# Theta and phi of an attention pair written in place by GpSimd and VectorE, with one copy a half, and a third part of the stage

## The chip, the cores and the metric

The kernel runs on one core of a Trainium2 chip. The metric is the time of one execution on the device in microseconds. The kernel before took 1916.14 us, the median of three runs.

## What is computed

32 images of 128 channels by 1024 pixels go through two attention layers, each 1024 queries by 1024 keys over the pixels of one image. The first layer, the one that the change touches, is:

```python
theta = _conv1x1(x, W_theta, b_theta)      # 64 channels of 128
phi   = _conv1x1(x, W_phi, b_phi)          # 64 channels of 128
f = jnp.einsum('ndq,ndk->nqk', t, p) * scale
f = jax.nn.softmax(f, axis=-1)
attn = jnp.einsum('nqk,nck->ncq', f, g).reshape(n, c, h, w)   # g is x
return x + _conv1x1(attn, W_fuse, b_fuse)
```

The second layer is a group norm over its input, then attention with q, k and v of 128 channels, a projection and the residual. Everything is wanted in float32 accuracy, so each operand of a product is split in a high part and a remainder, and a product is two or three matmuls.

## The kernel before, in words

**Slots.** One pass of the loop has 16 slots. In slots 0 to 7 the scores of the eight row tiles (128 queries by 1024 keys) of layer 0 of one image are made, in slots 8 to 15 those of layer 1 of the image before. Each of the five engines runs through the same slots in a `body` of its own and works on a tile some slots later than TensorE: VectorE's row maxima (`maxima`, L745) and ScalarE's exponentials (`exponentials`, L631) one slot after the scores. The order of work on an engine is that of the calls in its `body`; across engines there are only semaphores. The `body` functions stand at L430 (the DMA queue of SyncE, SP), L562 (TensorE, PE), L677 (ScalarE, ACT), L840 (VectorE, DVE) and L1012 (GpSimd, POOL).

**Tiles.** Scores lie in one of three parts of PSUM (`s_ps`, order in `PART`, L37). Four tiles are a group. Tiles 1 and 2 of a group go from ACT (`pair_hi`, L663) over DVE (`take_lo`, L753) to a DMA transpose (`transposes`, L353, and `move`, L359, on SP); tile 0 goes over POOL (`copied_lo`, L973) to the same; tile 3 is transposed by TensorE itself (`transposes`, L481) once its exponential is there, in the slot after its scores. The product with the values (`values`, L490) comes six slots after the first tile of the group, a quarter a slot, so the values of the tiles 12 to 15 begin in slot 2 of the next pass and those of the tiles 0 to 3 in slot 6.

**Units.** Between the scores TensorE makes one small product a slot, by the table `UNITS` (L54): for the image after, `tp0` in slot 10 and `tp1` in slot 12 are theta (rows 0 to 63) and phi (rows 64 to 127) of pixels 0 to 511 and 512 to 1023. ACT takes a unit from PSUM to one of the two parts of `stage` (`take_unit`, L597), and waits before that until the unit that had this part before is split (`until_stage_before`, L170). `tp0` and `tp1` both have part 0, `w0` (slot 7) before them and `v1` (slot 2 of the next pass) after them too. POOL splits the unit one slot later (`split_units`, L894): high part with `scaled` (L889), remainder with `rest` (L892).

**Theta and phi.** The scores of layer 0 are two matmuls a half, with both parts of theta stacked over the partitions against phi in both halves of the partitions:

```python
mm = product(out, [(theta2[:, qs], phi2[:, 0, ks]), (theta2[:, qs], phi2[:, 1, ks])])
```

So theta's high part stands in `theta2[0:64]` and its remainder in `theta2[64:128]`, while phi's high part and remainder stand in `phi2` twice, once in each 64 partitions. POOL writes all to a buffer `tp_hl` in their own partitions, and in slot 13 SP issues four DMAs (`tp_copies`, L416, the issues at L425 to L428) that bring phi to both places and theta to both places, 1.5 MB as the profile counts them. They wait for both splits and for the last score tile of layer 0 that reads the old ones. Scores of slot 0 (`scores`, L452) wait for all four (`s_tp_copy`).

**Around slot 0.** In slot 0 TensorE's order is: scores of tile 0, the group norm's first product (`gn1`, which needs mean and variance, the end of DVE's `statistics`, L809, in slot 15), the transposes of tile 15, values. On SP the order from slot 12 is: transpose of tile 10; slot 13: reciprocals out (L382), the four copies; slot 14: reciprocals in (L393), transpose of tile 12; slot 15: transpose of tile 13; slot 0: transpose of tile 14.

Of the kernel before, what the change touches and what calls it, by code (L numbers as in the profile page):

```python
# [7 lines left out]
F32 = mybir.dt.float32  # L8
F32R = mybir.dt.float32r
# [5 lines left out]
C = 128  # L15
D = 64
# [38 lines left out]
         12: "tp1", 14: "v0"}  # L55
STAGE = {"v1": 0, "k0": 1, "k1": 0, "q0": 1, "w0": 0, "q1": 1, "tp0": 0, "w1": 1, "tp1": 0, "v0": 1}

SPLIT_LAG = {"v1": 2, "k0": 1, "k1": 1, "q0": 1, "w0": 1, "q1": 1, "tp0": 1, "w1": 1, "tp1": 1, "v0": 1}
STAGES = 2
XR_SLOT = 0  # L60
XS_SLOT = 1
X_MAX_SLOT = 7
MX_SLOT = 9
X_SLOT = 8
# [3 lines left out]
RES_SLOTS = (5, 12)  # L68
TP_COPY_SLOT = 13
TP_COPIES = 4  # L70

# [9 lines left out]
def attention_pair(nc: bass.Bass, x, w_theta_t, w_phi_t, w_fuse_t, q_w_t, k_w_t, p_w_t, v_w, vectors,  # L81
# [88 lines left out]
    def until_stage_before(it, s):  # L170
# [5 lines left out]
        return value(lambda i: count(staged_at, 0, last(i) + 1), it)  # L176

    def place(s):

        return PAIRS - 1 if s % GROUP == COPIED and s // GROUP % 2 else s % GROUP  # L180
# [24 lines left out]
    with ExitStack() as ctx:  # L205
        def sb(name, shape, dt=F32):
            return ctx.enter_context(nc.sbuf_tensor(name, shape, dt))
# [30 lines left out]
        phi2 = sb("phi2", [C, 2, N], F32R)  # L238

        tp_hl = sb("tp_hl", [C, 2, N], F32R)  # L240
        q_hi, q_lo = sb("q_hi", [C, N], F32R), sb("q_lo", [C, N], F32R)
# [74 lines left out]
        s_den = sem("den_scaled_ready")  # L316
        s_tp_copy = sem("theta_phi_copied")
        s_split_hi = sem("unit_split_hi")
# [24 lines left out]
        def _(sp):  # L343
# [71 lines left out]

            def tp_copies(it, s):  # L416
                if s != TP_COPY_SLOT or not here(mx_at, it, MX_SLOT):
                    return
                sp.wait_ge(s_split, before(staged_at, it, s))
                sp.sem_inc(s_carrier)  # L420

                sp.wait_ge(s_scores, before(tile_at, it, PHASE))
                sp.sem_inc(s_carrier)
                theta_hl, phi_hl = (tp_hl[rows, :, :].bitcast(F32) for rows in (slice(0, D), slice(D, C)))
                sp.dma_start(phi2[0:D, :, :].bitcast(F32), phi_hl).then_inc(s_tp_copy, 16)  # L425
                sp.dma_start(phi2[D:C, :, :].bitcast(F32), phi_hl).then_inc(s_tp_copy, 16)
                sp.dma_start(theta2[0:D, :].bitcast(F32), theta_hl[:, 0, :]).then_inc(s_tp_copy, 16)  # L427
                sp.dma_start(theta2[D:C, :].bitcast(F32), theta_hl[:, 1, :]).then_inc(s_tp_copy, 16)  # L428

            def body(it):  # L430
                for s in range(SLOTS):
                    reciprocals_in(it, s)
                    transposes(it, s)
                    reciprocals_out(it, s)
                    image_loads(it, s)
                    stores(it, s)
                    tp_copies(it, s)

# [5 lines left out]
        def _(pe):  # L444
# [7 lines left out]
            def scores(it, s, half):  # L452
                if not here(tile_at, it, s):
                    return
                if half == 0:

                    last = part_before(it.like, s)
                    if last is not None and copied_at(last):
                        pe.wait_ge(s_exp, until_part_before(tile_at, it, s))
                    if last is not None and crossed_at(last):  # L460
                        pe.wait_ge(s_pair, until_part_before(crossed_at, it, s))
                    if last is not None and turned_at(last):
                        pe.wait_ge(s_tlo, until_part_before(turned_at, it, s))
                    if s == 0:
                        pe.wait_ge(s_tp_copy, 16 * TP_COPIES * before(mx_at, it, 0))
                    if s == PHASE:
                        pe.wait_ge(s_split, before(staged_at, it, 7))
                    if s == PHASE + GROUP:
                        pe.wait_ge(s_split, before(staged_at, it, 9))
# [118 lines left out]
        def _(act):  # L588
# [8 lines left out]
            def take_unit(it, s):  # L597
# [11 lines left out]

                act.wait_ge(s_split, until_stage_before(it, s))  # L610
                to = stage[:, STAGE[name], :]
                if name[0] == "v":
# [87 lines left out]
        def _(dve):  # L700
# [119 lines left out]
            def x_maxima(it, s):  # L820
                if s != X_MAX_SLOT or not here(x_at, it, X_SLOT):
# [6 lines left out]
                                        apply_absolute_value=True).then_inc(s_x_max, 1)  # L828

            def bound_to_scale(it, s):  # L830
                s = s - 1
                if here(mx_at, it, s):
                    value_scale(0, before(mx_at, it, s) + 1)
# [6 lines left out]
            def body(it):  # L840
                for s in range(SLOTS):
                    take_bounds(it, s)
                    maxima(it, s)
                    normalised(it, s)
                    take_lo(it, s)
                    reciprocals(it, s)
                    bound_to_scale(it, s)
                    x_maxima(it, s)
                    statistics(it, s - 2, 0)
                    statistics(it, s - 1, 1)  # L850
# [27 lines left out]
        def _(pool):  # L878
# [15 lines left out]
            def split_units(it, s):  # L894
# [7 lines left out]
                if name[0] == "t":  # L902

                    pool.wait_ge(s_tp_copy, 16 * TP_COPIES * or_none(before(mx_at, it, s) - 1))
                    hi, lo = (tp_hl[:, n, half * HALF:(half + 1) * HALF] for n in range(2))
                    hi_read = hi.bitcast(F32)
# [150 lines left out]
```

## Time and profile before

| | us |
|---|---|
| median of three runs | 1916.14 (1911.53 to 1922.02) |
| the profiled execution, whole | 1910.44 |
| its span, first to last instruction | 1908.6 |
| TensorE's matmuls, busy | 1738.8 |
| VectorE, ScalarE, GpSimd, busy | 1383.4, 1404.0, 1379.7 |

Of TensorE's idle time the largest piece by far is ended by the DMA that fills theta. The clock that TensorE was granted was 0.961 of full speed in the mean. A table of busy time says little here, as all engines are between 72% and 91%; what counts is the piece of a pass in which TensorE stands still, and what came last there. TensorE's `gn1` product occurs once a pass, so its start times mark the passes: those at 81.7 and 1794.3 us are 30 passes apart.

### The profile page before, as it was taken

To read this page: it belongs to the slowest core of one execution; us is meant where nothing else is said; L and a number is where in the kernel's file an instruction comes from. 1 tells how busy PE (TensorE), PEld (TensorE's weight loads), DVE (VectorE), ACT (ScalarE), POOL (GpSimd) and SP (SyncE) were. 2 spreads that over 40 slices of the span, in tenths; PEclk is the share of its full clock that TensorE was granted. 3 is DMA by queue.
4 is the path that set the end of the run, shared out by engine and by line. 5 is a ranking of instruction groups with operands and counts; after the bars stand their busy time and mean duration, and the time that the engine had idled before them with its cause. 6 is when DMAs were issued, how large, how long until landed. Compare 5 with 4: busy or idle time off the path is not lost.

```text
span 1908.6 us, 34400 instructions
## 1 busy us (share of the span) xinstructions
PE 1738.8 (91%) x8970; PEld 1141.4 (60%) x8970; DVE 1383.4 (72%) x1541; ACT 1404.0 (74%) x2088; POOL 1379.7 (72%) x1449
## 2 busy tenths in 40 slices
PE   4699999999999999999999999999999999999996
PEld 3456656666665666656666565666666666656653
DVE  4478777778777778777778777778777777777764
ACT  3378777778777778777778777778777777877764
POOL 3468766778777778776778776778776778876754
PEclk9799999999999999999999999999999999999999
DMA  4588888898988988888988898888888988888874
GB/s 91 117 161 167 173 177 173 173 176 163 179 178 172 176 174 168 179 176 173 179 173 168 178 180 172 184 173 171 173 178 176 187 169 177 168 170 175 173 140 94
DMA packets 861110, 319.89 MB, mean 168 GB/s; under 512 B 823328, under 2 KB 824224, under 8 KB 856992
## 3 DMA queue, kind: packets, MB, share of 16 engines
q1 hardware_dynamic: 861088, 319.64, 84.0%
q8 instruction: 9, 0.15, 0.0%
q14 instruction: 13, 0.11, 0.0%
HBM read 50.86 MB, written 17.04 MB: 36 GB/s over the span
## 4 chain that ended last, share of the span: by engine, by line
PE 42%; issue 14%; DMA 11%; POOL 11%; ACT 9%; SPq 6%; DVE 4%; POOLq 0%; ACTq 0%; DVEq 0%
PE o_ps L449 15%; PE s_ps L449 15%; DMA theta<-tp_hl 10%; PE m_ps L449 6%; PE s_ps L487 6%; SPq L427 3%; ACT s_ps L649 3%; POOL x_lo L892 2%; ACT et L659 2%; DVE den_scaled L779 2%; ACT h_hi L628 2%; ACT e L649 2%; DVE neg_max L750 1%; POOL tp_hl L892 1%; POOL y_sb L996 1%
## 5 line engine op out<-in xcount | busy, mean ns | idle before, releaser
L750 DVE TENSOR_REDUCE neg_max<-s_ps 128x1 f32<-128x1024 f32 x512 | 625.5, 1222 | 226.4 <-PE s_ps L449 222.6
L449 PE MATMUL o_ps<-et,v_hi 128*128 128x512 f16 x2048 | 709.9, 388 | 20.5 <-issue 10.8
L449 PE MATMUL s_ps<-phi,theta 128*128 128x512 f32 x1024 | 343.3, 460 | 108.9 <-DMA theta<-tp_hl 99.7
L449 PE MATMUL o_ps<-et,v_lo 128*128 128x512 f16 x1024 | 396.7, 387 | 0.0
L449 PEld LDWEIGHTS o_ps<-et,v_hi 128*128 128x128 f16 x2048 | 206.5, 101 | 265.7 <-issue 83.3
L767 DVE SCALAR_TENSOR_TENSOR pair<-s_ps,pair 128x1024 f16<-128x1024 f32 x256 | 312.0, 1219 | 38.5 <-ACT pair L674 37.2
L649 ACT ACTIVATE s_ps<-s_ps,neg_max 128x1024 f32<-128x1024 f32 x256 | 278.0, 1086 | 79.5 <-DVE neg_max L750 77.9
L449 PEld LDWEIGHTS s_ps<-phi,theta 128*128 128x128 f32 x1024 | 201.8, 201 | 184.1 <-DMA theta<-tp_hl 102.6
L892 POOL TENSOR_TENSOR pair<-e_copied,pair 128x1024 f16<-128x1024 f32 x128 | 274.2, 2142 | 22.2 <-ACT pair L672 22.2
L761 DVE SCALAR_TENSOR_TENSOR et<-s_ps,et 128x1024 f16<-128x1024 f32 x128 | 156.8, 1225 | 180.0 <-ACT et L659 180.0
L674 ACT ACTIVATE pair<-s_ps 128x1024 f16<-128x1024 f32 x256 | 262.2, 1024 | 17.6
L449 PE MATMUL s_ps<-k_hi,q_hi 128*128 128x512 f32 x512 | 248.6, 486 | 4.5 <-POOL q_lo L892 2.1
L449 PE MATMUL s_ps<-k_hi,q_lo 128*128 128x512 f32 x512 | 202.7, 396 | 0.0
L449 PE MATMUL s_ps<-k_lo,q_hi 128*128 128x512 f32 x512 | 200.8, 392 | 0.0
L659 ACT ACTIVATE et<-s_ps 128x1024 f16<-128x1024 f32 x128 | 131.1, 1024 | 71.8 <-PE s_ps L487 65.4
L649 ACT ACTIVATE e<-s_ps,neg_max 128x1024 f32<-128x1024 f32 x128 | 142.8, 1115 | 48.4 <-DVE neg_max L750 48.2
L487 PE MATMUL s_ps<-ident_sb,e 128*128 128x128 f32 x1024 | 155.0, 301 | 12.1 <-ACT e L649 12.1
L487 PEld LDWEIGHTS s_ps<-ident_sb,e 128*128 128x128 f32 x1024 | 135.5, 159 | 37.9 <-ACT e L649 27.0
L892 POOL TENSOR_TENSOR v_lo<-stage,v_hi 128x512 f16<-128x512 f32 x128 | 148.2, 1158 | 10.7
L649 ACT ACTIVATE e_copied<-s_ps,neg_shifted 128x1024 f32<-128x1024 f32 x128 | 143.0, 1117 | 4.1
L449 PEld LDWEIGHTS o_ps<-et,v_lo 128*128 128x128 f16 x1024 | 102.7, 100 | 71.5 <-issue 5.0
L672 ACT ACTIVATE pair<-e_copied 128x1024 f16<-128x1024 f32 x128 | 135.3, 1057 | 9.2
(130 smaller groups left out, 2849.2 us busy)
## 6 DMA issues: line engine op xcount, KB each, us to landing
phi<-tp_hl SPq DMA_DIRECT2D x64, 512.0 KB, 5.4
rden_row<-rden_dram SPq DMA_DIRECT2D x128, 256.0 KB, 4.5
xs<-in_x SPq DMA_DIRECT2D x32, 512.0 KB, 4.8
theta<-tp_hl SPq DMA_DIRECT2D x64, 256.0 KB, 7.1
out_y<-y_sb SPq DMA_DIRECT2D x64, 256.0 KB, 3.5
et<-pair SPq DMA_TRANSPOSE x384, 4.5
rden_dram<-rden SPq DMA_DIRECT2D x128, 2.0 KB, 2.0
w_f<-in_w_fuse_t SPq DMA_DIRECT2D x1, 64.0 KB, 2.4
```

The source lines that it names most:

```text
L427: sp.dma_start(theta2[0:D, :].bitcast(F32), theta_hl[:, 0, :]).then_inc(s_tp_copy, 16)
L449: mm = pe.matmul(out, lhs_t, rhs, start=start and n == 0, stop=stop and n == len(terms) - 1)
L487: mm = pe.transpose(s_ps[:, part(t), kb * P:(kb + 1) * P], e[:, kb * P:(kb + 1) * P], ident[:, :])
L628: nc.scalar.activation(h_hi[:, :], x1[:, :], ACT.Identity, scale=gn_a[:, 0:1], bias=gn_b[:, 0:1]).then_inc(s_hhi, 1)
L649: nc.scalar.activation(to[:, :], s_ps[:, r, :], ACT.Exp, bias=bias, accum_out=den[:, g, t % GROUP:t % GROUP + 1]).then_inc(s_exp, 1)
L659: nc.scalar.activation(et[:, t // GROUP % 4, TURNED, 0:KB, :], s_ps[:, part(t), :].rearrange("k (b q) -> k b q", b=KB), ACT.Copy, scale=E_ ...
L672: nc.scalar.activation(pair[:, r, 0, :], e_copied[:, :], ACT.Copy).then_inc(s_copied_hi, 1)
L674: nc.scalar.activation(pair[:, r, 0, :], s_ps[:, part(t), :], ACT.Copy, scale=E_SCALE).then_inc(s_pair_hi, 1)
L750: nc.vector.tensor_reduce(neg_max[:, t % 4:t % 4 + 1], s_ps[:, part(t), :], AX.X, ALU.max, negate=True).then_inc(s_max, 1)
L761: nc.vector.scalar_tensor_tensor(out=blocks[:, KB:2 * KB, :], in0=s_ps[:, part(t), :].rearrange("k (b q) -> k b q", b=KB), scalar=E_SCALE, ...
L767: nc.vector.scalar_tensor_tensor(out=pair[:, r, 1, :], in0=s_ps[:, part(t), :], scalar=E_SCALE, in1=pair[:, r, 0, :], op0=ALU.mult, op1=AL ...
L892: nc.gpsimd.tensor_tensor(out, in_, hi, ALU.subtract).then_inc(sem, 1)
```

## The change

Theta and phi are written to `theta2` and `phi2` themselves, and `tp_hl` is gone. For each half POOL writes theta's high part to `theta2[0:64]` with one more instruction, then splits the whole unit into `phi2` (its rows 64 to 127 are phi; rows 0 to 63 get theta's parts, which nobody reads). DVE computes theta's remainder into `theta2[64:128]`, in slots 12 (`tp0`) and 14 (`tp1`). SP copies phi's two parts from rows 64 to 127 to rows 0 to 63 with one DMA of 256 KB a half, in slots 12 (`tp0`) and 13 (`tp1`). POOL's writing waits until the last score tile of layer 0 is made. `tp0` gets a part of `stage` of its own, a third one, and ACT waits for DVE's remainders before it overwrites a part from which they are computed.

```diff
-STAGE = {... "tp0": 0, "w1": 1, "tp1": 0, "v0": 1}
+STAGE = {... "tp0": 2, "w1": 1, "tp1": 0, "v0": 1}
-STAGES = 2
+STAGES = 3
-TP_COPY_SLOT = 13
-TP_COPIES = 4
+THETA_LO_SLOTS = {12: "tp0", 14: "tp1"}
+PHI_SLOTS = {12: "tp0", 13: "tp1"}
...
-            def tp_copies(it, s):
-                if s != TP_COPY_SLOT or not here(mx_at, it, MX_SLOT):
-                    return
-                sp.wait_ge(s_split, before(staged_at, it, s))
+            def phi_copies(it, s):
+                unit = unit_slot(PHI_SLOTS.get(s))
+                if unit is None or not here(tp_at, it, unit):
+                    return
+                half = int(UNITS[unit][-1])
+                cols = slice(half * HALF, (half + 1) * HALF)
+                sp.wait_ge(s_split, before(staged_at, it, unit) + 1)
                 sp.sem_inc(s_carrier)
-
-                sp.wait_ge(s_scores, before(tile_at, it, PHASE))
-                sp.sem_inc(s_carrier)
-                theta_hl, phi_hl = (tp_hl[rows, :, :].bitcast(F32) for rows in (slice(0, D), slice(D, C)))
-                sp.dma_start(phi2[0:D, :, :].bitcast(F32), phi_hl).then_inc(s_tp_copy, 16)
-                sp.dma_start(phi2[D:C, :, :].bitcast(F32), phi_hl).then_inc(s_tp_copy, 16)
-                sp.dma_start(theta2[0:D, :].bitcast(F32), theta_hl[:, 0, :]).then_inc(s_tp_copy, 16)
-                sp.dma_start(theta2[D:C, :].bitcast(F32), theta_hl[:, 1, :]).then_inc(s_tp_copy, 16)
+                sp.dma_start(phi2[0:D, :, cols].bitcast(F32), phi2[D:C, :, cols].bitcast(F32)).then_inc(s_phi, 16)
...
                     if s == 0:
-                        pe.wait_ge(s_tp_copy, 16 * TP_COPIES * before(mx_at, it, 0))
+                        pe.wait_ge(s_phi, 16 * before(tp_at, it, 0))
+                        pe.wait_ge(s_theta_hi, before(tp_at, it, 0))
+                        pe.wait_ge(s_theta_lo, before(tp_at, it, 0))
...
                 act.wait_ge(s_split, until_stage_before(it, s))
+                if name in ("tp0", "v1"):
+
+                    act.wait_ge(s_theta_lo, before(tp_at, it, s))
...
+            def theta_lo(it, s):
+                unit = unit_slot(THETA_LO_SLOTS.get(s))
+                if unit is None or not here(tp_at, it, unit):
+                    return
+                name, n = UNITS[unit], before(tp_at, it, unit)
+                half = int(name[-1])
+                cols = slice(half * HALF, (half + 1) * HALF)
+                dve.wait_ge(s_theta_hi, n + 1)
+                nc.vector.tensor_tensor(theta2[D:C, cols], stage[0:D, STAGE[name], :], theta2[0:D, cols].bitcast(F32),
+                                        ALU.subtract).then_inc(s_theta_lo, 1)
...
                     bound_to_scale(it, s)
+                    theta_lo(it, s)
                     x_maxima(it, s)
...
-                    pool.wait_ge(s_tp_copy, 16 * TP_COPIES * or_none(before(mx_at, it, s) - 1))
-                    hi, lo = (tp_hl[:, n, half * HALF:(half + 1) * HALF] for n in range(2))
+                    pool.wait_ge(s_scores, before(tile_at, it, PHASE))
+                    cols = slice(half * HALF, (half + 1) * HALF)
+                    scaled(theta2[0:D, cols], src[0:D, :], 1.0, 1.0, ALU.mult, ALU.mult).then_inc(s_theta_hi, 1)
+
+                    hi, lo = phi2[:, 0, cols], phi2[:, 1, cols]
                     hi_read = hi.bitcast(F32)
```

`phi_copies` takes the place of `tp_copies` at the end of SP's slot.

## Rows read from the trace of the kernel before

**Rows 1.** The page: span, and TensorE's busy time, share, instructions.

```profile
span 1908.6 us, 34400 instructions
PE 1738.8 (91%) x8970; PEld 1141.4 (60%) x8970; DVE 1383.4 (72%) x1541; ACT 1404.0 (74%) x2088; POOL 1379.7 (72%) x1449
```

**Rows 2.** TensorE's waits from 81.7 to 1794.3 us: total us, times, longest.

```profile
PE s_ps L449 <- DMA theta<-tp_hl: 91.0, 30, 4.5
PE o_ps L449 <- issue: 5.8, 9, 1.0
```

**Rows 3.** Stretches: length, busy by engine (PE first), granted clock, DMA share, GB/s.

```profile
81.70:1794.30 1712.60, 1604.16 (x8357) 1059.27 (x8356) 1284.53 (x1405) 1312.13 (x1949) 1290.20 (x1348) 0.97 0.87 174
425.50:483.50 58.00, 55.15 (x282) 36.14 (x281) 42.81 (x47) 43.86 (x65) 43.15 (x45) 0.94 0.85 172
1394.80:1450.70 55.90, 51.95 (x282) 34.32 (x281) 41.95 (x47) 43.94 (x65) 43.11 (x45) 1.00 0.89 178
```

**Rows 4.** TensorE's waits in the single pass from 1394.8 to 1450.7 us.

```profile
PE s_ps L449 <- DMA theta<-tp_hl: 2.8, 1, 2.8
PE o_ps L449 <- issue: 1.1, 2, 0.7
```

**Rows 5.** Timeline around slot 0: TensorE's start, length, line, tiles, idle before.

```profile
820.58 0.38 PE L449 MATMUL o_ps<-et,v_hi 128*128 128x512 f16 x1
824.47 1.20 PE L449 MATMUL s_ps<-phi,theta 128*128 128x512 f32 x4 [3.51 <-DMA theta<-tp_hl]
825.64 1.52 PE L487 MATMUL s_ps<-ident_sb,e 128*128 128x128 f32 x8
```

**Rows 6.** Timeline of SP's queue, same pass.

```profile
814.90 0.51 SPq L425 DMA_DIRECT2D phi<-tp_hl  x1
...
818.01 2.50 SPq L428 DMA_DIRECT2D theta<-tp_hl  x1
820.77 1.08 SPq L393 DMA_DIRECT2D rden_row<-rden_dram  x1
822.10 8.64 SPq L368 DMA_TRANSPOSE et<-pair  x3
```

**Rows 7.** The first copy of phi: duration of its issue, and time to landing.

```profile
L425 SPq DMA_DIRECT2D phi<-tp_hl x32: 472/508/549, 19.4 to 1782.9; - x32
...
DMA to landing us min/median/max: 4.2/4.2/4.3
```

**Rows 8.** The page's DMA issues: KB each, median us from issue to landing.

```profile
rden_row<-rden_dram SPq DMA_DIRECT2D x128, 256.0 KB, 4.5
```

**Rows 9.** Timeline of GpSimd, slots 11 to 14 of the same pass.

```profile
807.20 0.62 POOL L889 TENSOR_SCALAR tp_hl<-stage 128x512 fp32r<-128x512 f32 x1
...
812.37 1.28 POOL L892 TENSOR_TENSOR tp_hl<-stage,tp_hl 128x512 fp32r<-128x512 f32 x1
816.17 1.27 POOL L986 TENSOR_TENSOR x<-x,xr 128x512 f32<-128x512 f32 x1 [2.53 <-DVE x L804]
817.40 2.14 POOL L892 TENSOR_TENSOR pair<-e_copied,pair 128x1024 f16<-128x1024 f32 x1
```

**Rows 10.** Timeline of VectorE, same pass.

```profile
812.54 1.13 DVE L779 SCALAR_TENSOR_TENSOR den_scaled<-den,v_scale,e_factors 128x4 f32<-128x4 f32 x1
...
815.04 1.05 DVE L804 TENSOR_TENSOR x<-o_ps,rden_row 128x512 f32<-128x512 f32 x1
816.01 1.22 DVE L750 TENSOR_REDUCE neg_max<-s_ps 128x1 f32<-128x1024 f32 x1
...
818.68 0.68 DVE L814 BATCH_NORM_STATS2 stats<-x 128x6 f32<-128x512 f32 x1
...
820.02 1.23 DVE L750 TENSOR_REDUCE neg_max<-s_ps 128x1 f32<-128x1024 f32 x1 [0.29 <-issue]
...
829.48 0.21 DVE L779 SCALAR_TENSOR_TENSOR den_scaled<-den,v_scale,e_factors 128x4 f32<-128x4 f32 x1
```

**Rows 11.** Timeline of ScalarE, same pass: the end of tile 15's exponential.

```profile
822.38 0.19 ACT L649 ACTIVATION_READ_ACCUMULATOR e<-s_ps,neg_max 128x1 f32 x1
```

More of the change, by code:

```diff
@@ L55 @@
          12: "tp1", 14: "v0"}
-STAGE = {"v1": 0, "k0": 1, "k1": 0, "q0": 1, "w0": 0, "q1": 1, "tp0": 0, "w1": 1, "tp1": 0, "v0": 1}
+STAGE = {"v1": 0, "k0": 1, "k1": 0, "q0": 1, "w0": 0, "q1": 1, "tp0": 2, "w1": 1, "tp1": 0, "v0": 1}
 SPLIT_LAG = {"v1": 2, "k0": 1, "k1": 1, "q0": 1, "w0": 1, "q1": 1, "tp0": 1, "w1": 1, "tp1": 1, "v0": 1}
-STAGES = 2
+STAGES = 3
 XR_SLOT = 0
@@ L62 @@
 X_MAX_SLOT = 7
-MX_SLOT = 9
 X_SLOT = 8
@@ L176, in until_stage_before, with unit_slot @@
         return value(lambda i: count(staged_at, 0, last(i) + 1), it)
+    def unit_slot(name):
+        return next((s for s, unit in UNITS.items() if unit == name), None)
     def place(s):
@@ L238, in attention_pair @@
         phi2 = sb("phi2", [C, 2, N], F32R)
-        tp_hl = sb("tp_hl", [C, 2, N], F32R)
         q_hi, q_lo = sb("q_hi", [C, N], F32R), sb("q_lo", [C, N], F32R)
@@ L316, in attention_pair @@
         s_den = sem("den_scaled_ready")
-        s_tp_copy = sem("theta_phi_copied")
+        s_theta_hi, s_theta_lo = sem("theta_hi_ready"), sem("theta_lo_ready")
+        s_phi = sem("phi_twice")
         s_split_hi = sem("unit_split_hi")
@@ L436, in body @@
                     stores(it, s)
-                    tp_copies(it, s)
+                    phi_copies(it, s)
             iterations(sp, body, first=-1)
```

## The prediction

> **What bounds the kernel now.** I read the page first. TensorE is busy for 91% of 1908.6 us and the three others for 72% to 74% [rows 1], so the question is what TensorE's idle time is made of. The table of its waits over the 30 steady passes (81.7 to 1794.3 us) answers: 91.0 us in 30 waits, one a pass, are ended by the DMA that fills theta; the next kind is 5.8 us in nine waits [rows 2]. So 3.03 us a pass, and all in one place. The timeline of TensorE shows the place: after the values of slot 15, issued at 820.58 and some 0.4 us long, it stands for 3.51 us before the scores of slot 0 [rows 5].
>
> The wait has a second price. The table by stretches gives the granted clock: 1.00 in some passes, 0.94 in others, 0.97 over all 30 [rows 3]. In the pass shown the transposes right after the wait take 1.52 us for eight [rows 5]; it is TensorE at 1.2 instead of 2.4 GHz, just after it stood still. A clock of 0.97 over 1712.6 us costs 51 us (43 to 60, as the figure is rounded), 1.7 us a pass.
>
> A pass now takes 1712.6 / 30 = 57.09 us. Without the theta wait and at full clock 57.09 - 3.03 - 1.7 = 52.36 us are left. A single pass says the same: the one from 1394.8 us ran at 1.00, took 55.9 us and had 2.8 us of theta wait [rows 3, 4], which leaves 53.1, of which 1.1 us are two waits at values products with no cause shown [rows 4]. So TensorE's own work in a pass is close to 52.0 us, and that is the floor.
>
> **What the change removes.** The last of the four copies is issued at 818.01, lasts 2.50 us on SP's queue, and TensorE goes on at 824.47; the first had been issued at 814.90 [rows 5, 6]. All four are serial on one queue, and phi's first, 512 KB, lands 4.2 us after its issue [rows 7]. Now only phi's copy of 256 KB a half is left. The one of `tp0` goes in slot 12, the one of `tp1` in slot 13 at the place of the four. The second needs POOL's split of `tp1`, whose remainder now ends at 812.37 + 1.28 = 813.65 [rows 9]. POOL gets one more high part before each half; 0.62 us is the row of a 128x512 one [rows 9], and two of them move that end to about 814.9. So the second copy is issued near 815.0, where the first of the four was. I take its landing at 4.2 us as phi's first, which is twice its size [rows 7], and 4.5 us as another 256 KB DMA [rows 8] for the upper end: it lands at 819.2 to 819.5. TensorE wants it at about 821.0 (820.58 and the last values). It is 1.5 us early, and the theta wait goes to nothing. Half the partitions make no difference to that: phi's first copy also runs over 64 of them. The Trainium skill (SBUF — State Buffer, on concurrent DMAs and ports) says that only a transfer over all 128 partitions reaches all ports, so that a copy from 64 to 64 partitions would be slow for its size; the row of 4.2 us is such a copy and has this in it.
>
> SP's queue gets free earlier too. Behind the four copies were the reciprocals (820.77) and the three transposes of the tiles 12 to 14, from 822.10 for 8.64 us [rows 6]. Tile 12 is ready when POOL's remainder ends, 817.40 + 2.14 = 819.5 [rows 9].
>
> **What it adds, on POOL.** Two high parts, 2 x 0.62 us a pass. POOL stood idle for 2.53 us ahead of L986 in slot 14 [rows 9], which comes right behind, so nothing on the path moves. If that cover were gone, 1.24 us would go into the mean and variance that `gn1` needs. The added wait for the scores of layer 0 is over since slot 8. Behind it on POOL stands only work of slot 11 and later. ACT's waits for theta's remainders look at work done at least four slots before (`v1` in slot 2 after slot 14), and `tp1` no longer waits for the split of `tp0`, which was not TensorE's wait in any row; I count both as nothing.
>
> **What it adds, on DVE.** Two subtractions of 64x512, both operands in SBUF. No row has this form. From below: a two-operand instruction on 128x4 takes 0.21 us [rows 10]. From above: L804 on 128x512, with an operand in PSUM and a strided one, takes 1.05 us [rows 10]. Nearest is the statistics instruction, 128x512 out of SBUF, at 0.68 us [rows 10], and I take 0.7. By the formula in the Trainium skill (VectorE: DVE Perf Modes, fp32 `tensor_tensor`) it would be 0.69 us; no run here shows it yet.
>
> The one in slot 12 lies before tile 12's maximum, whose exponential waits for ACT anyway: nothing. The one in slot 14 follows L804 directly, at 816.0, and behind it are, in order, tile 14's maximum (816.01), tile 13's remainder, the statistics (818.68), and tile 15's maximum (820.02) [rows 10]. The 0.29 us that DVE had to spare there cover part of it; tile 15's exponential, now over at 822.38 + 0.19 = 822.57 [rows 11], moves to about 823.0.
>
> **What is late next.** TensorE starts slot 0 at about 821.0. From the scores to the transposes of tile 15, with `gn1` between, it took 825.64 - 824.47 = 1.17 us [rows 5], so it stands before the transposes at 822.15. These need that exponential, over at 823.0, and some 0.1 us for the semaphore. So a wait of 0.95 us appears, now hidden under the theta wait (without the subtraction it would be 0.5). Its bounds are 0.5 and, if DVE gives way to POOL once (1.27 us, below), 2.2. `gn1` needs the statistics at about 820.3: no wait. The rest of DVE's and ACT's chain is a little closer behind TensorE for the next slots, and the transposes of the tiles 12 to 14 must have landed by slot 2. The pass from 1394.8 shows what happens where the clock does not fall: 1.1 us of waits at values products, which a slower TensorE did not have [rows 4]. They can be the landing of transposes. Over all passes the waits other than theta's that are in the 52.36 are already 0.4 us. I add 0.7 us for the passes that had none of them; the bounds are 0 and 1.5.
>
> **Sum.** 52.36 + 0.75 (the 0.95 less some 0.2 that such waits cost now) + 0.7 = 53.8 us a pass, against 57.09: 3.3 us, times 30 = 99 us. The first theta wait is longer, outside these 30 passes, with POOL's split the last before it: there the end moves from 824.47 to 819.2 as above, less 0.6 for POOL: 4.7 us. Together 104 us. The profiled execution took 1910.44 us, of which 1.8 are outside its span; 1910.4 - 104 = 1806. The median of the runs shown is 5.7 us higher. I say 1808.
>
> **The rivals.**
> *Nothing new waits.* DVE's subtraction fits in gaps, the transposes come in time, because the DMA queues carry 0.5 MB instead of 1.5 MB: 52.4 us a pass, 4.7 x 30 + 4.7 = 146 us less, 1765. For it: the DMA share was 0.87 and falls. Against it: the exponential of tile 15 is late by 0.5 us even in the rows as they stand. 0.12.
> *The clock falls all the same.* A wait and a lower clock go together [rows 5], but not strictly: the pass from 1394.8 us ran at 1.00 with a wait of 2.8 us in it [rows 3, 4], and the mean wait of a pass is no longer than 3.03 us. If about 1 us before the transposes is enough, 1.7 us a pass are kept: 55.5 us, 1910.4 - 48 - 5 = 1857. Against it: waits up to 1.0 us at values products are in passes with a clock of 1.00. 0.15.
> *DVE and POOL block one another (slower).* The 128x4 instruction that takes 0.21 us alone took 1.13 us from 812.54, and ended at 813.67, just when POOL's subtraction begun at 812.37 ended, 813.65 [rows 9, 10]. So DVE with both operands in SBUF waits for a POOL instruction in progress. If the subtraction of slot 14 lost not once but to L986 and to L892 right after it (816.17 to 819.5), it would be 3.5 us late; tile 15's exponential with it, so TensorE would wait 4.5 us in slot 0, with the low clock again: 52.36 + 4.3 + 0.7 + 1.7 = 59.1, 2.0 us a pass more, 1910 + 55 = 1965. It decides from a delay of 2.4 us on. Against it: L804 of DVE ends at 816.09 and releases L986 at 816.17, so DVE's next instruction starts first; and DVE got in when one POOL instruction had ended [rows 9, 10]. The Trainium skill (SBUF — State Buffer, on who interferes with whom) has it as an exclusive lock, held for the whole instruction by whichever starts first, for DVE with two SBUF inputs against a POOL instruction that reads SBUF; the rows of 1.13 against 0.21 us agree. 0.06.
> *It doesn't do what it says.* The second copy lands too late, and the theta wait becomes a phi wait of about the same length: it would have to take 9.5 us from its issue at 815.0, where the rows show 4.2 and 4.5. About 1905. 0.04.
>
> **How the numbers follow.** The forecast has 0.63, with the rivals 0.12, 0.15, 0.06 and 0.04. A measurement of this kernel can tell about 0.5%, 10 us, from no change. Faster by more: 0.63 + 0.12 + 0.15 = 0.90; within: 0.04; slower: 0.06. The forecast's own bounds: waits of 0.5 and 0 give 52.7 us a pass, 1775; 2.2 and 1.5 give 55.9, 1870. For 8 times in 10 I take 1770 to 1860, which holds the forecast, most of the clock rival, and leaves out most of the case with nothing new.
>
> **What would show it.** Each step: TensorE's waits no longer name a DMA of theta, and phi's copies are released well before slot 0; a wait of 0.5 to 1.5 us a pass stands before the transposes (L487 of before), ended by ACT's exponential; DVE's new instruction lasts about 0.7 us and starts within 0.1 us of the end of L804 in slot 14; POOL's idle time ahead of L986 shrinks by about 1.2 us; the granted clock is 0.99 or more; a pass takes 53.8 us. The prediction would be wrong if the clock falls with a wait of 1 us, or if values products in the slots 2 and 6 wait for transposes for more than 1.5 us a pass.

## The result, and the profile after

The changed kernel takes 1783.43 us (median, 1780.63 to 1784.94) beside 1916.43 us for the kernel before: a ratio of 0.9303, 95% interval 0.9275 to 0.9332. It is 7% faster, where 1808 us was forecast. The profiled execution took 1780.63 us against 1910.44, so it is there that 129.8 us have to be found.

The page of the changed kernel, first lines, then the DMA issues with their median time to landing:

```profile
span 1778.8 us, 34679 instructions
PE 1686.0 (95%) x8970; PEld 1112.1 (63%) x8970; DVE 1414.7 (80%) x1605; ACT 1399.3 (79%) x2088; POOL 1442.2 (81%) x1513
...
phi<-phi SPq DMA_DIRECT2D x64, 256.0 KB, 3.1
...
et<-pair SPq DMA_TRANSPOSE x384, 4.5
```

TensorE's waits over the 30 steady passes, which now run from 76.9 to 1668.9 us, and the row of that stretch (length, busy by engine, granted clock, DMA share, GB/s):

```profile
PE s_ps L487 <- ACT e L652: 16.4, 44, 1.2
PE o_ps L447 <- issue: 11.9, 23, 1.3
PE o_ps L447 <- POOL k_lo L907: 2.5, 2, 1.3
```
```profile
76.90:1668.90 1592.00, 1556.07 (x8358) 1032.09 (x8357) 1311.90 (x1465) 1307.40 (x1948) 1349.05 (x1408) 1.00 0.85 167
```

Beside [rows 2, 3]: the 91.0 us of theta waits are gone and no DMA of phi has taken their place. The transposes by TensorE now wait 16.4 us for ScalarE's exponential: 11.6 us of it in slot 0, before those of tile 15 (29 waits, 0.39 us a pass), the rest in slot 4, before those of tile 3. Values products wait 11.9 us with no cause in this view: 5.6 us in slot 2 and 6.3 us in slot 6. The clock is 1.00 instead of 0.97. A pass takes 1592.0 / 30 = 53.07 us instead of 57.09, which is 120.6 of the 129.8 us. The start of the first of these passes moved from 81.7 to 76.9 us, 4.8 us. The piece behind the last of them is 109.9 instead of 114.3 us long; the clock that fell after the last theta wait belongs to that piece, so it is the same gain once more.

Slot 0 of one pass, to be held against [rows 5, 6, 9 to 11]: first TensorE, then SP, then GpSimd, VectorE and ScalarE, each with start, length, line and tiles, and in brackets the idle time before.

```profile
819.42 1.27 PE L447 MATMUL s_ps<-phi,theta 128*128 128x512 f32 x4
820.54 0.28 PE L530 MATMUL m_ps<-mean_var,group_avg_sb 128*128 128x2 f32 x2
821.17 1.09 PE L487 MATMUL s_ps<-ident_sb,e 128*128 128x128 f32 x8 [0.35 <-ACT e L652]
...
828.06 0.39 PE L447 MATMUL o_ps<-et,v_hi 128*128 128x512 f16 x1
```
```profile
810.90 0.76 SPq L426 DMA_DIRECT2D phi<-phi  x1
...
813.59 0.60 SPq L426 DMA_DIRECT2D phi<-phi  x1
...
818.34 6.59 SPq L370 DMA_TRANSPOSE et<-pair  x3
```
```profile
812.22 1.28 POOL L907 TENSOR_TENSOR phi<-stage,phi 128x512 fp32r<-128x512 f32 x1
814.29 1.77 POOL L1004 TENSOR_TENSOR x<-x,xr 128x512 f32<-128x512 f32 x1 [0.79 <-DVE x L807]
```
```profile
811.34 0.29 DVE L782 SCALAR_TENSOR_TENSOR den_scaled<-den,v_scale,e_factors 128x4 f32<-128x4 f32 x1
...
813.14 1.07 DVE L807 TENSOR_TENSOR x<-o_ps,rden_row 128x512 f32<-128x512 f32 x1
814.24 0.69 DVE L841 TENSOR_TENSOR theta<-stage,theta 64x512 fp32r<-64x512 f32 x1
...
818.57 1.22 DVE L753 TENSOR_REDUCE neg_max<-s_ps 128x1 f32<-128x1024 f32 x1 [0.29 <-PE s_ps L447]
```
```profile
820.92 0.19 ACT L652 ACTIVATION_READ_ACCUMULATOR e<-s_ps,neg_max 128x1 f32 x1
```

TensorE goes from slot 15 to the scores of slot 0 without a gap. The second copy is issued when GpSimd's split ends (812.22 + 1.28 = 813.50, issue at 813.59) and lands 3.1 us later, at 816.7, 2.7 us early. The exponential of tile 15 ends at 821.11 and the transposes start at 821.17. The three DMA transposes behind the copies begin 2.2 us before `gn1` and take 6.59 us of SP's queue, where they took 8.64; this pass is at the low end, over the 30 passes the median is 7.2 us, against 8.5 us before.

### The profile page after: what moved, and what is told of

The parts are those of the page before. It is cut to its first block, busy times and chain, and to the rows that moved or that the text cites. A ratio compares the mean times of both kernels' runs of the same rounds, so it can differ in the third digit from the quotient of the medians.

```text
span 1778.8 us, 34679 instructions
## 1 busy us (share of the span) xinstructions
PE 1686.0 (95%) x8970; PEld 1112.1 (63%) x8970; DVE 1414.7 (80%) x1605; ACT 1399.3 (79%) x2088; POOL 1442.2 (81%) x1513
## 4 chain that ended last, share of the span: by engine, by line
PE 66%; issue 13%; DVE 8%; ACT 7%; POOL 2%; DMA 1%; ACTq 0%; SPq 0%; DVEq 0%; POOLq 0%
PE o_ps L447 26%; PE s_ps L447 22%; PE m_ps L447 11%; PE s_ps L487 7%; DVE neg_max L753 3%; DVE pair L770 2%; ACT e L652 2%; ACT s_ps L652 2%; ACT h_hi L631 1%; DVE stats L817 1%; ACT et L662 1%; DMA et<-pair 1%; DVE den_scaled L782 1%; DVE x L807 0%; DVE theta L841 0%
## 5 line engine op out<-in xcount | busy, mean ns | idle before, releaser
L447 PE MATMUL o_ps<-et,v_hi 128*128 128x512 f16 x2048 | 696.6, 382 | 28.3 <-issue 18.2
L447 PE MATMUL o_ps<-et,v_lo 128*128 128x512 f16 x1024 | 389.8, 381 | 0.0
L447 PEld LDWEIGHTS o_ps<-et,v_hi 128*128 128x128 f16 x2048 | 202.9, 99 | 269.8 <-issue 78.4
L447 PE MATMUL s_ps<-phi,theta 128*128 128x512 f32 x1024 | 332.1, 447 | 12.5 <-ACT e_copied L652 4.8
L447 PEld LDWEIGHTS s_ps<-phi,theta 128*128 128x128 f32 x1024 | 197.2, 194 | 73.5 <-ACT e_copied L652 6.2
L487 PE MATMUL s_ps<-ident_sb,e 128*128 128x128 f32 x1024 | 136.1, 276 | 23.3 <-ACT e L652 22.4
L487 PEld LDWEIGHTS s_ps<-ident_sb,e 128*128 128x128 f32 x1024 | 114.8, 140 | 51.4 <-ACT e L652 40.5
```

The costliest lines, as they stand in the source:

```text
L447: mm = pe.matmul(out, lhs_t, rhs, start=start and n == 0, stop=stop and n == len(terms) - 1)
L487: mm = pe.transpose(s_ps[:, part(t), kb * P:(kb + 1) * P], e[:, kb * P:(kb + 1) * P], ident[:, :])
```

## The experiments

**First question: was it the wait?** The theory on record books the gain as theta wait plus clock. The rival is that the copies cost something else as well: bytes in the DMA queues and time of SP's queue ahead of the transposes. Four runs on one chip, with the kernel before at 1906.08 us.

**e1, the kernel before without the wait.** Edit to the kernel before (the scores of tile 0 read constant tiles, so this part of the computation is left out):

```diff
-                    if s == 0:
+                    if s == 1:
                         pe.wait_ge(s_tp_copy, 16 * TP_COPIES * before(mx_at, it, 0))
...
+                if s == 0:
+                    mm = product(out, [(theta_f[:, qs], phi_f[:, 0, ks]), (theta_f[:, qs], phi_f[:, 1, ks])])
```

> The kernel before with its four copies as they are, but TensorE waits for them in slot 1 instead of slot 0: the scores of tile 0 of layer 0 are computed from constant tiles (theta_f, phi_f), so their content is left out of the computation. Traffic, GpSimd's and VectorE's work and SP's order stay those of before. Theory (the gain is the wait of 3.0 us a pass and the clock that it costs): the theta wait is gone or under 0.5 us, the clock is 0.99, a pass takes 53.0 to 54.0 us, the median 1785 to 1815 us. Rival (the gain comes from 1 MB a pass less in the DMA queues and from SP's queue being free 4 us earlier, so that transposes land in time): a pass stays above 55.5 us, the median above 1860, with waits at the values products of slot 2 instead.

Measured: 1913.06 us, ratio to before 1.002 (0.9992 to 1.0048). The theory missed by 100 us, and the rival's bound was kept. TensorE's waits from 73.6 to 1851.7 us, SP's queue, and TensorE in the same pass (`gn1` at 879.84):

```profile
PE o_ps L451 <- issue: 96.4, 30, 3.8
PE s_ps L491 <- ACT e L654: 9.8, 31, 1.3
```
```profile
875.38 2.53 SPq L430 DMA_DIRECT2D theta<-tp_hl  x1
878.17 1.10 SPq L395 DMA_DIRECT2D rden_row<-rden_dram  x1
879.53 8.12 SPq L370 DMA_TRANSPOSE et<-pair  x3
```
```profile
890.39 0.39 PE L451 MATMUL o_ps<-et,v_hi 128*128 128x512 f16 x1 [3.03 <-issue]
```

The theta wait is gone from the steady passes, and a wait of 3.2 us a pass stands in slot 2, before the first values product of the tiles 12 to 15. The clock is no better than before, 0.95 from 82 to 1660 us. This view names no cause ("issue"). The view of the line of the DMA transposes does: over the same stretch it lists who waited for them, and narrowed to the last of the three in this pass it gives its start, 885.9 us, and its time to landing:

```profile
  PE o_ps L451: 96.8, 31
```
```profile
L370 SPq DMA_TRANSPOSE et<-pair x1: 1765/1765/1765, 885.9 to 885.9; - x1
DMA to landing us min/median/max: 4.3/4.3/4.3
```

It lands at 890.2 us and TensorE goes on at 890.39. In each of the 27 passes of e1 between 76 and 1670 us for which all is in the trace that product starts 0.18 to 0.21 us after this landing. The same holds in all 14 kernels of this document: their traces have 306 waits at values products between 76 and 1670 us that are put down to "issue" or to a DMA transpose, and each ends 0.18 to 0.38 us after a DMA transpose lands.

**e2, half a MB of traffic added.** The changed kernel with two copies of 256 KB from a constant tile to a spare one behind phi's second copy; their own semaphore is awaited one pass later.

```diff
+                if half == 1:
+                    sp.dma_start(spare[0:D, :].bitcast(F32), spare_src[:, 0, :].bitcast(F32)).then_inc(s_spare, 16)
+                    sp.dma_start(spare[D:C, :].bitcast(F32), spare_src[:, 1, :].bitcast(F32)).then_inc(s_spare, 16)
```

> The changed kernel plus the two DMAs of 256 KB that theta had before, from a constant tile to a spare one, issued behind phi's second copy in slot 13 and awaited by nobody but themselves a pass later. Theory (the wait, not the traffic): SP's queue is blocked for some 4.4 us as before, ends at about where the transposes of slot 14 start now, and the transposes land a little later: +0 to +1 us a pass, median 1783 to 1815. Rival (the traffic and the queue were the price): back to 1860 or more.

Measured: 1784.87 us, 0.9351 (0.9313 to 0.9388), no change of time that can be told from the changed kernel. In the trace the bytes are not free: the three transposes behind them take 7.7 us of SP's queue in the median instead of 7.2, the last lands 0.4 us later against `gn1`, and the wait in slot 2 grows from 0.2 to 0.4 us a pass. The expected blocking of SP by 4.4 us did not come: the two issues took 0.49 and 0.63 us, where theta's in the kernel before took 1.88 and 2.50 behind two copies of 512 KB. So the length of an issue on SP was no property of the copy alone; it went with what had been queued in front of it.

**e3, theta in place, phi by two DMAs of 512 KB.** In slot 13, from a buffer:

```diff
-PHI_SLOTS = {12: "tp0", 13: "tp1"}
+PHI_SLOTS = {13: "tp1"}
...
-                sp.dma_start(phi2[0:D, :, cols].bitcast(F32), phi2[D:C, :, cols].bitcast(F32)).then_inc(s_phi, 16)
+                sp.dma_start(phi2[0:D, :, :].bitcast(F32), tp_hl[D:C, :, :].bitcast(F32)).then_inc(s_phi, 16)
+                sp.dma_start(phi2[D:C, :, :].bitcast(F32), tp_hl[D:C, :, :].bitcast(F32)).then_inc(s_phi, 16)
```

> Theta in place as in the changed kernel, but phi from a buffer by the two DMAs of 512 KB of the kernel before, both in slot 13. By the rows of before the second lands 7.1 us after the first is issued. The theory: first issue 5.8 us before TensorE wants slot 0, so a phi wait of about 1.4 us in slot 0, which hides the wait for tile 15's exponential (0.5 us): +0.9 us a pass, and with a clock of 0.99 the median is near 1812; if a wait of 1.4 us is enough for the clock to fall, 1.7 to 1.9 us more a pass, near 1868. Rival (only theta's copies were late): as the changed kernel, 1783.

Measured: 1834.56 us, 0.9624 (0.9579 to 0.967). TensorE's largest wait and the stretch from 82 to 1660 us:

```profile
PE s_ps L449 <- DMA theta<-tp_hl: 82.3, 27, 4.5
```
```profile
PE s_ps L451 <- DMA phi<-tp_hl: 54.2, 28, 2.3
```
```profile
82.00:1660.00 1578.00, 1507.59 (x8058) 996.66 (x8057) 1272.06 (x1411) 1263.24 (x1879) 1300.16 (x1357) 0.99 0.85 172
```

The first line is the kernel before in the same stretch, the others are e3. The phi wait is 1.9 us a pass, not 1.4, and the clock stays at 0.99; the time lies between the two that were expected. So theta in place with phi left to the DMA is worth a little over half of the gain.

**e4, phi's second copy one slot later.** `PHI_SLOTS = {12: "tp0", 14: "tp1"}`, behind the transpose of tile 12.

> The changed kernel with phi's second copy in slot 14 of SP instead of 13, so behind the transpose of tile 12, which waits for GpSimd's remainder. Theory (what matters is where the last copy stands in SP's order against slot 0): it is issued 7 us later, lands 17.7 to 19 us after the mark at which slot 0 wants it at 13.4, a phi wait of 4.3 to 5.5 us, the clock falls in most passes, a pass takes 58 to 60 us and the median is 1930 to 1990, slower than before. Rival (SP's order does not matter, the smaller copies do): within 1% of the changed kernel.

Measured: 1956.51 us, 1.0257 (1.0215 to 1.0299): slower than the kernel before, by the order on SP alone. SP and TensorE in one pass, and the stretch:

```profile
831.37 1.84 SPq L370 DMA_TRANSPOSE et<-pair  x1
833.40 1.01 SPq L426 DMA_DIRECT2D phi<-phi  x1
```
```profile
837.34 2.07 PE L447 MATMUL s_ps<-phi,theta 128*128 128x512 f32 x4 [4.54 <-DMA phi<-phi]
```
```profile
82.00:1660.00 1578.00, 1445.34 (x7496) 959.56 (x7495) 1189.12 (x1316) 1173.68 (x1745) 1211.10 (x1260) 0.96 0.76 151
```

The wait and the clock came as expected (4.5 us a pass, 0.96).

**Second question: what is the second price of the copies?** After e1 the theory was changed: behind the theta wait lies a second one of the same length, for the transposes that are queued behind the copies; both must go. e5 puts the missing 1 MB back into the changed kernel, awaited by nobody:

```diff
+                    sp.dma_start(spare[0:D, :, :].bitcast(F32), spare_src[:, :, :].bitcast(F32)).then_inc(s_spare, 16)
+                    sp.dma_start(spare[D:C, :, :].bitcast(F32), spare_src[:, :, :].bitcast(F32)).then_inc(s_spare, 16)
```

> The changed kernel plus two DMAs of 512 KB from a constant tile to a spare one, issued on SP behind phi's second copy in slot 13 and awaited by nobody until a pass later: the 1.5 MB a pass of the kernel before, with nothing waiting for the added part. The first theory (only the theta wait counted) fell with the run in which TensorE no longer waited for theta and then stood 3.2 us a pass in slot 2. New theory: behind the theta wait lay a second one of the same length, for the transposes of the tiles 12 to 14, which are queued behind the copies; 1 MB more in front of them brings it back: their issue ends 7 us or more after gn1 instead of 4.4, a wait of 2 to 3.5 us in slot 2, a pass of 55.5 to 57.5 us, median 1860 to 1915. Rival (the run with 0.5 MB more cost nothing, so traffic in front of the transposes is free, and what the wait-free variant of before lost came from elsewhere): under 1800.

Measured: 1917.15 us, 1.0062 (1.0041 to 1.0083), 2 us above the expected range; the clock is 0.95 from 82 to 1660 us. All of the gain is gone, with theta and phi in place and nobody waiting for the added bytes. SP and TensorE (`gn1` at 876.75):

```profile
871.32 0.49 SPq L433 DMA_DIRECT2D spare<-spare_src  x1
871.85 0.62 SPq L434 DMA_DIRECT2D spare<-spare_src  x1
872.73 2.15 SPq L398 DMA_DIRECT2D rden_row<-rden_dram  x1
875.13 9.49 SPq L373 DMA_TRANSPOSE et<-pair  x3
```
```profile
887.41 0.60 PE L456 MATMUL o_ps<-et,v_hi 128*128 128x512 f16 x1 [3.06 <-issue]
```

The transposes begin 1.6 us before `gn1`, where they began 2.2 us before it in the changed kernel, and last 9.49 us. Over the passes the medians are 10.0 instead of 7.2 us of SP's queue, and the last lands 10.6 instead of 7.5 us after `gn1`. So of the 3.0 us of delay 0.6 are SP getting to them later, and the rest is that they are slower with 1.5 MB in front of them. The wait in slot 2 is 3.2 us a pass and ends 0.2 us after that landing, as in e1.

**e11, the same 1 MB in slot 10.** The two issues moved from slot 13 to slot 10 of SP, ahead of the transposes of the tiles 8 to 10 (`if s != 10 or not here(mx_at, it, 9): return` in a function of their own).

> The same two added DMAs of 512 KB as in the run with full traffic, but issued on SP in slot 10, before the transposes of the tiles 8 to 10, where the trace of the changed kernel shows a DMA share of 0.6. Theory (it is the place of the bytes, in front of the transposes of the tiles 12 to 14 that layer 0's short slots give little time, and not their number): the wait in slot 2 does not come back, 0 to +1 us a pass, median 1783 to 1815. Rival (the DMA engines are near full over the whole pass, so 1 MB more costs wherever it stands): 1860 to 1915, as with the copies in slot 13.

Measured: 1836.91 us, 0.9646 (0.9608 to 0.9685). Neither expectation holds. The trace shows both at work:

```profile
824.20 0.52 SPq L436 DMA_DIRECT2D spare<-spare_src  x1
824.78 0.58 SPq L437 DMA_DIRECT2D spare<-spare_src  x1
826.81 10.76 SPq L373 DMA_TRANSPOSE et<-pair  x3
```
```profile
840.32 0.52 PE L460 MATMUL o_ps<-et,v_hi 128*128 128x512 f16 x1 [1.38 <-issue]
```

Again the transposes behind the added bytes are stretched, to 10.76 us here, and in the median to 11.2 us where the same group took 7.1 in the changed kernel; the last of them lands 3.5 us later against `gn1`. The values product of their group, now in slot 14, waits for 1.38 us here and 1.6 us a pass in the mean, so this group had almost 2 us to spare and the one of slot 2 had nothing. 1 MB cost in both places in front of a group, and the place decided how much.

**Third question: the new wait before the transposes of tile 15.** Theory: it is set by VectorE's chain from slot 13 on. e6 to e8 ran on one chip (before: 1906.82 us), e9 and e10 on a second (1909.36 us), e12 on a third with e11 (1903.02 us).

**e6, VectorE's subtraction of slot 14 twice**, the first time into a spare tile, `if half == 1:` in front of the old one.

> The changed kernel with VectorE's subtraction of slot 14 done twice, the first time into a spare tile. Theory (VectorE's chain from slot 14 to tile 15's maximum ends TensorE's wait in slot 0, 0.53 us a pass now): 0.69 us more on VectorE become 0.5 to 0.7 us more a pass, median 1799 to 1806. Rival (VectorE has slack there): 1783, within 0.3%.

Measured: 1826.85 us, 0.9587 (0.9563 to 0.9611), some 43 us more than the changed kernel where 16 to 23 were expected. VectorE and GpSimd in one pass, and TensorE's wait from 82 to 1660 us:

```profile
828.11 1.07 DVE L808 TENSOR_TENSOR x<-o_ps,rden_row 128x512 f32<-128x512 f32 x1
829.10 0.68 DVE L843 TENSOR_TENSOR spare<-stage,theta 64x512 fp32r<-64x512 f32 x1
829.79 1.67 DVE L845 TENSOR_TENSOR theta<-stage,theta 64x512 fp32r<-64x512 f32 x1
```
```profile
829.25 1.66 POOL L1008 TENSOR_TENSOR x<-x,xr 128x512 f32<-128x512 f32 x1 [0.29 <-DVE x L808]
830.87 2.59 POOL L911 TENSOR_TENSOR pair<-e_copied,pair 128x1024 f16<-128x1024 f32 x1
```
```profile
PE s_ps L488 <- ACT e L653: 68.5, 58, 2.2
```

The first subtraction, right behind L808, goes through in 0.68 us and GpSimd's L1008 is held up (1.66 us, where it took 1.27 [rows 9] and 1.77 in the changed kernel). The second is asked for with L1008 under way: it takes 1.67 us and ends at 831.46, while GpSimd's ends at 830.91, so 0.55 of its 0.69 us of work lie behind that. GpSimd's next is stretched in turn, from 2.14 to 2.59. So one more instruction of 0.69 us added 1.7 us to VectorE's chain, and the wait in slot 0 rose by 1.6 us a pass, from 0.39 to 2.0.

**e7, GpSimd's high part of theta in slot 13 twice**, the first time into a spare tile.

> The changed kernel with GpSimd's high part of theta in slot 13 done twice, the first time into a spare tile: +0.61 us. Theory (GpSimd's addition is covered by its idle time of 0.6 to 0.8 us ahead of the addition of the residual in slot 14, and phi's copy lands 1.5 us early): 1783, within 0.3%. Rival (phi's copy or the mean and variance are at the edge): +0.3 us or more a pass, median 1792 or more.

Measured: 1789.18 us, 0.9387 (0.936 to 0.9414). Against the 0.9303 and 0.9327 of the changed kernel that is slower by 0.6% to 0.9%. One of the two intervals of the changed kernel overlaps with this one, so the times alone say little, but the trace shows that the theory (within 0.3%) missed. GpSimd was still idle for 0.58 us ahead of L1007, so it was not late. VectorE and GpSimd in slot 13:

```profile
812.96 1.22 DVE L783 SCALAR_TENSOR_TENSOR den_scaled<-den,v_scale,e_factors 128x4 f32<-128x4 f32 x1
```
```profile
812.97 0.61 POOL L905 TENSOR_SCALAR theta<-stage 64x512 fp32r<-64x512 f32 x1
813.55 0.62 POOL L905 TENSOR_SCALAR spare<-stage 64x512 fp32r<-64x512 f32 x1
```

VectorE's instruction of 0.21 us on 128x4 takes 1.22 us here and ends at 814.18, with GpSimd's second instruction (814.17); in the changed kernel it took 0.29. All its operands lie in SBUF, and it stands at the head of VectorE's chain for slot 14. Over 28 passes of e7 it took 0.91 us in the mean, in 28 of the changed kernel 0.41, and TensorE's wait in slot 0 was longer by just that (0.91 against 0.40).

**e8, theta's remainder of `tp1` on GpSimd** instead of VectorE:

```diff
+                if name == "tp1":
+                    pool.wait_ge(s_split, n + 1)
...
+                    rest(theta2[D:C, cols], src[0:D, :], theta2[0:D, cols].bitcast(F32), s_theta_lo)
+                    pool.wait_ge(s_theta_lo, before(tp_at, it, s) + 1)
```

> The changed kernel with theta's remainder of tp1 computed by GpSimd in slot 13, behind phi's remainder, instead of by VectorE in slot 14 (tp0's stays with VectorE). Theory: tile 15's maximum is 0.7 us earlier, the wait in slot 0 falls from 0.53 to under 0.2 us a pass; GpSimd has 1.3 us more, of which 0.5 come back since its residual addition in slot 14 is no longer held up by VectorE (1.77 to 1.27 us) and 0.7 are idle: median 1768 to 1778. Rival (the wait has another cause, or GpSimd becomes late for the statistics): 1783 or more.

Measured: 1793.71 us, 0.9419 (0.9374 to 0.9465), no gain, and in the rival's range (1783 or more). The trace shows the first half of the theory right in direction only, and why it gives nothing. TensorE's waits of e8 from 82 to 1660 us:

```profile
PE o_ps L447 <- issue: 27.3, 40, 2.5
PE s_ps L487 <- ACT e L652: 9.2, 30, 1.0
```

In that stretch the waits for an exponential fell from 16.4 to 9.2 us, those in slot 0 from 0.39 to 0.28 us a pass, not to under 0.2 as expected; so most of the wait before the transposes of tile 15 was not the subtraction's. GpSimd's residual addition is back at 1.27 us, as forecast. The waits at values products rose from 11.9 to 27.3 us: GpSimd's remainder for tile 12 ends later, the three transposes begin 1.7 us before `gn1` in the median instead of 2.2, the last of them lands 0.6 us later, and the wait in slot 2 grows from 0.2 to 0.8 us a pass.

**e9, two parts of the stage** (`"tp0": 0`, `STAGES = 2`, and ScalarE waits for theta's remainder at `tp1` too).

> The changed kernel with two parts of the stage as before: tp0 in part 0 again, and ScalarE waits before taking tp1 until tp0 is split and VectorE has computed its remainder. Theory (the third part is covered: in the changed kernel ScalarE takes tp1 some 0.1 us before GpSimd ends the split of tp0): 0 to +0.15 us a pass, median 1783 to 1788, no change. Rival (the third part carries a part of the gain): +0.3 us or more a pass, 1792 or more.

Measured: 1779.64 us, 0.9334 (0.9302 to 0.9366). The ratio is within 0.4% of that of the changed kernel (0.9303 and 0.9327), so no gain of the third part can be told.

**e10, the load of the next image in slot 4** (`XS_SLOT = 4`).

> The changed kernel with the load of the next image (512 KB) moved on SP from slot 1 to slot 4, behind the transposes of the tiles 0 to 2 instead of in front. Theory (the waits of 0.4 us a pass at the values product of slot 6, for which the profile shows no cause, are the landing of these transposes, held up by the load): they go, -0.2 to -0.4 us a pass, median 1771 to 1778. Rival (the load then comes late for VectorE's maximum over it in slot 7, which holds up its queue): 1783 or more, with a wait of VectorE at that maximum.

Measured: 1775.63 us, 0.931 (0.9277 to 0.9344). The median is in the expected range, but the changed kernel in e12 is as fast, so no gain is shown. The trace says more: the waits in slot 6 for which the load was moved (6.3 us over the 30 passes of the changed kernel, 2.6 us in e12) are gone, and instead there are ten waits, 3.7 us, in slot 10, for the group of transposes that the load now stands in front of. The load's price was moved, not removed.

**e12, the changed kernel again.**

> The changed kernel itself once more, beside the same runs of the kernel before, as a yardstick for the runs that differ from it by less than 1%. Both theories: ratio 0.927 to 0.935, a pass of 53.1 us.

Measured: 1776.42 us, 0.9327 (0.9289 to 0.9365). The same kernel gave ratios of 0.9303 and 0.9327 on two chips, so differences below 0.5% between runs on different chips say nothing here.

## Why the prediction was right, and what it had not seen

The time was inside the range, 25 us below the forecast. (The sum as written gives 1806 us for the profiled execution and 1812 us for the median; 1808 was said.) The rival that nothing new waits, at 1765 us, came nearer, 18 us off, though not its condition: the wait in slot 0 did appear. By its own steps:

**The theta wait goes to nothing: right, but for one more reason than the sum gave.** The copy was early by 2.7 us, not 1.5, as 256 KB landed in 3.1 us and not 4.2. The step that was incomplete is the one after it, "SP's queue gets free earlier too", which had no number. e1 takes the theta wait away and leaves the copies: no gain. e5 leaves everything in place and puts 1 MB back: the gain is lost. The sum booked 3.03 us of wait and 1.7 us of clock on the wait's account alone, yet either limit, theta's landing or the landing of the transposes behind 1.5 MB, is enough to hold a pass at 57 us. The changed kernel lifts both with the same bytes, so the sum came out. That it came out although one of its two limits had no number was in part luck: the bytes that the second limit needed gone went by the same edit. The trace of before held the hint. The last transpose of the pass in [rows 6] starts at 828.75 and lands 4.3 us later, at 833.0; 0.2 us behind that TensorE could have begun the values product of slot 2, and, kept back by 3.5 us of wait and the slow clock, it began it at 834.1. The cover was 0.9 us wide there and 0.8 us in the median, against a wait of 3.03 us. In the changed kernel there is no cover. In the pass shown the last transpose has these lines, so it lands at 827.9, and the product starts at 828.06:

```profile
L370 SPq DMA_TRANSPOSE et<-pair x1: 1395/1395/1395, 823.5 to 823.5; - x1
DMA to landing us min/median/max: 4.3/4.3/4.3
```

In 27 of the 30 passes the product starts 0.2 us after the landing, so the landing paces TensorE in slot 2. Against a start right behind the product before it (0.11 us apart, as in the kernel before) it comes 0.2 us later in the median and 0.4 us in the mean; half of that shows as idle time.

**The clock: right.** It is 1.00 in 28 of the 30 steady passes; the first ran at 0.90, as it did in the kernel before. In the one from 235.2 us (0.97) it fell to half for 3.4 us behind a wait of 1.31 us in slot 2; two waits of 1.29 and 1.35 us in others did not make it fall. So the rival that it falls all the same did not come true, but the waits that are left are close to where it does.

**The added work on GpSimd and VectorE.** The subtraction takes 0.69 us (0.7 taken), and it starts 0.03 us after L807's end, as forecast; the formula of the Trainium skill (VectorE: DVE Perf Modes) gives 0.69 us, and the trace agrees. GpSimd's idle time ahead of the residual's addition shrank from 2.53 to 0.79 us (1.2 us less forecast, 1.7 measured). Not forecast: that addition itself grew from 1.27 to 1.77 us, held by VectorE (in e8, without the subtraction, it took 1.27). The growth is not free: GpSimd's remainder for tile 12 comes right behind, ends at 816.02 + 2.15 = 818.17, and the DMA transposes start at 818.34. What it costs can be no more than the delay in slot 2, 0.4 us a pass in the mean (above).

**What is late next: right in place, too large in size.** The wait before the transposes of tile 15 was put at 0.95 us and measured 11.6 / 30 = 0.39. VectorE was not late for tile 15 in the pass shown: it waits 0.29 us for TensorE's scores. What is left there is the latency of maximum and exponential behind scores that now end without a gap, and e8, with 0.28 us and no subtraction in slot 14, says the same. The allowance for values products, 0.7 us on top of 0.4, measured 0.5 us in all. All waits of the steady passes sum to 1.1 us a pass, where the forecast of 53.8 had 1.8 over its floor of 52.0; that is the difference between 53.8 and 53.07 us, and over 30 passes 22 of the 25 us. The floor itself held: 53.07 - 1.1 = 52.0. The rest is mostly the tail, which is 4.4 us shorter.

**The third stage part and the split of phi's copy.** The former was counted as nothing, and e9 shows no difference from that. e3 shows that a DMA of phi in two pieces of 512 KB would have been worth only a ratio of 0.96.

**The slower rival** did not come true, but its mechanism is real: e6 shows VectorE delayed by one GpSimd instruction, and e7 by two in a row, where the argument against it had VectorE get in after the first. The lock of the Trainium skill (SBUF — State Buffer, on who interferes with whom) is what these rows show, 1.67 us against 0.69, and 1.22 against 0.21. The point from which it would have decided, 2.4 us of delay in slot 14, was not reached.

**Open.** That the waits at values products end with the landing of a DMA transpose is in the traces (e1); no run took only that wait away from the kernel before. Why 0.5 MB in front delays that landing by 0.4 us and 1 MB by 3.0 us is not shown.

## What to carry to other kernels

A wait that ends last can hide a second one of the same length: before its whole length is booked, take the next thing that the waiting engine needs, and compute when it lands with the engine moved forward. A DMA that nobody waits for still has a price, in what is queued behind it; ask of each copy what lands after it, and on which deadline. And an instruction of VectorE with both operands in SBUF is to be costed with the GpSimd instruction that is under way when it starts, not alone.

## What the runs showed of the hardware

- 1 MB of added copies in front of three DMA transposes stretched their issue from 7.2 to 10.0 us (e5, slot 13) and from 7.1 to 11.2 us (e11, slot 10), medians over the passes; the last landed 3.0 and 3.5 us later. 0.5 MB (e2) made 7.7 us and a landing 0.4 us later, and the time showed no change.
- TensorE went on 0.18 to 0.38 us after the landing of the transpose that it waited for, in 306 waits.
- The issue time on SP went with the backlog: the same kind of 256 KB copy took 0.5 to 0.6 us in e2, and 1.9 to 2.5 us behind two of 512 KB.
- VectorE on 128x4 with its operands in SBUF took 0.21 us alone [rows 10] and 1.22 us with two GpSimd instructions of 0.61 us back to back (e7); it did not get in between them.
- The mean clock from 82 to 1660 us was 1.00 in the changed kernel, 0.99 with one wait of 1.9 us a pass in slot 0 (e3), 0.97 with 3.0 us (before), 0.96 with 4.5 us (e4), and 0.95 with 3.2 us in slot 2 (e1, e5). So it does not follow the length of the wait alone; in the kernel before, the stretch from 1394.8 us has 1.00 and a wait of 2.8 us, and the one from 425.5 us has 0.94 [rows 3, 4] and a wait of 2.7 us.
